# Three edge sweeps of a graph network: all rows gathered by GpSimd, and one multiplication for sixteen scaled copies

## The reference

```python
# layer 0 (1 head) and layer 1 (4 heads, with edge terms): attention
h = x @ W
alpha = leaky_relu(a_src[src] + a_dst[dst] (+ a_edge))
alpha = exp(alpha - segment_max(alpha, dst)[dst])
out   = segment_sum(alpha[:, None] * h[src], dst) / segment_sum(alpha, dst)
# layer 2: sums of edge attributes, then three dense layers
agg   = segment_sum(edge_attr_128, dst)
# layer 3: messages by relation
h     = einsum('nd,rdo->rno', x, W_rel)
agg   = segment_sum(h[edge_type, src], dst) / deg
```

## Time and profile before

| | us |
|---|---|
| median of 3 runs | 9807.24 (9797.97 to 9817.08) |
| span of the profiled execution | 9691.9 |
| first stage | 324.2 |
| sweep A, first gather to last join | 2242.5 |
| node stage after it | 384.0 |
| sweep B | 3141.5 |
| node stage after it | 434.2 |
| sweep R | 3012.6 |
| the rest | 152.9 |

### The profile page before, as it was taken

One profiled execution on the slowest core, in us unless ns is written; L12 is line 12 of the kernel. 1 busy time (PEld: TensorE's weight loads), 2 busy tenths in 40 slices (PEclk: granted clock), 3 DMA queues, 4 the chain that ended last, 5 costly groups with the idle time before them and its releaser, 6 DMA issues.

```text
span 9691.9 us, 57509 instructions
## 1 busy us (share of the span) xinstructions
PE 645.5 (7%) x2460; PEld 429.5 (4%) x2460; DVE 3381.8 (35%) x6204; ACT 1028.8 (11%) x3093; POOL 4970.1 (51%) x5237
## 2 busy tenths in 40 slices
PE   1100000000140000000000000580000000000000
PEld 1000000000140000000000000240000000000000
DVE  6555555555563222222222222761111111111113
ACT  1222222222120000000000000460000000000000
POOL 5766666666457444444444444216444444444445
PEclk7555555555565555555555555795555555555555
DMA  4456666666433222222222222452222222222222
GB/s 158 145 178 199 194 186 196 192 193 202 155 108 94 67 72 70 69 73 69 73 70 72 70 71 69 164 200 71 64 67 66 68 68 68 65 70 68 68 68 97
DMA packets 344911, 1045.34 MB, mean 108 GB/s; under 512 B 111529, under 2 KB 139564, under 8 KB 306594
## 3 DMA queue, kind: packets, MB, share of 16 engines
q1 hardware_dynamic: 157746, 670.54, 19.3%
q0 software_dynamic: 172192, 365.19, 14.8%
q10 hardware_dynamic: 14544, 5.93, 0.3%
HBM read 527.27 MB, written 513.96 MB: 107 GB/s over the span
## 4 chain that ended last, share of the span: by engine, by line
SPq 36%; issue 31%; DVE 14%; another core or an unknown queue 8%; PE 3%; POOL 3%; ACT 3%; ACTq 1%; DMA 1%; DVEq 0%; POOLq 0%
SPq L250 21%; SPq L249 7%; SPq L247 7%; DVE ps L1256 2%; DVE ps L1281 2%; POOL node_sums L1387 1%; DVE edge_rows L1286 1%; ACT edge_rows L1220 1%; DVE edge_rows L1264 1%; PE ps L2028 1%; ACTq L250 1%; DVE edge_logit L1356 1%; DVE feat_prod L1343 1%; DVE fine L592 1%
## 5 line engine op out<-in xcount | busy, mean ns | idle before, releaser
L1158 POOL DMA_INDIRECT edge_rows<-table_b,src_i x1523 | 1440.8, 946 | 1642.7 <-DMA sums_b<-edge_rows 1161.0
L2113 POOL DMA_INDIRECT edge_rows<-table_rel,rel_row x1523 | 1440.7, 946 | 1641.1 <-DMA sums_rel<-edge_rows 1096.3
L1158 POOL DMA_INDIRECT edge_rows<-table_a,src_i x1568 | 1485.0, 947 | 702.8 <-issue 487.3
L2197 DVE TENSOR_TENSOR edge_rows<-edge_rows,ps 128x1024 f32<-128x1024 f32 x195 | 237.9, 1220 | 2301.3 <-DMA edge_rows<-table_rel 2220.7
L1286 DVE TENSOR_TENSOR edge_rows<-edge_rows,ps 128x1032 f32<-128x1032 f32 (+1 forms) x390 | 484.2, 1241 | 962.5 <-remote 726.8
L1350 DVE TENSOR_TENSOR edge_rows<-edge_rows,ps 128x2112 f32<-128x2112 f32 (+1 forms) x99 | 230.9, 2332 | 1010.1 <-ACT ps L1223 961.8
L1220 ACT ACTIVATE edge_rows<-edge_rows,weight_decay 128x129 f32<-128x129 f32 x1560 | 493.6, 392 | 211.5 <-issue 211.3
L1281 DVE TENSOR_TENSOR ps<-edge_rows,ps 128x1032 f32<-128x1032 f32 (+1 forms) x390 | 485.6, 1245 | 8.6 <-issue 1.9
L1316 DVE TENSOR_TENSOR z<-edge_rows,dst_logit 128x16 f32<-128x16 f32 (+2 forms) x198 | 40.1, 203 | 1194.2 <-DMA edge_rows<-table_b 1171.4
L1223 ACT ACTIVATE ps<-weight_decay 128x128 f32<-128x128 f32 (+1 forms) x99 | 27.7, 280 | 3036.5 <-DVE weight_decay L1337 1562.8
L2144 ACT ACTIVATE ps<-keep 128x16 f32<-128x16 f32 x98 | 19.6, 201 | 2985.8 <-issue 1534.7
(11 more groups left out here) (296 smaller groups left out, 3207.3 us busy)
## 6 DMA issues: line engine op xcount, KB each, us to landing
sums_a<-edge_rows SPq DMA_DIRECT2D x98, 2064.0 KB
sums_b<-edge_rows SPq DMA_DIRECT2D x98, 1120.0 KB, 4.2
edge_rows<-in_ea SPq DMA_DIRECT2D x98, 1024.0 KB
sums_rel<-edge_rows SPq DMA_DIRECT2D x98, 1024.0 KB, 3.9
table_rel<-rel SPq DMA_DIRECT2D x98, 512.0 KB
edge_rows<-table_b SPq DMA_DIRECT2D x2880, 0.5 KB
edge_rows<-table_b ACTq DMA_DIRECT2D x2880, 0.5 KB
edge_rows<-table_rel ACTq DMA_DIRECT2D x2880, 0.5 KB
```

The source lines that it names most:

```text
L1158: e.indirect_dma_start(out=rows[:, s, i, 0:L.W], out_offset=None, in_=L.table, in_offset=bass.IndirectOffsetOnAxis(ap=src[:, at:at + 1], a ...
L2113: e.indirect_dma_start(out=rows[:, s, i, :], out_offset=None, in_=table_rel, in_offset=bass.IndirectOffsetOnAxis(ap=rel_row[:, at:at + 1], ...
```

## The change

`Helped` is gone with its tables, registers, transposes and semaphores; `Gathers`, in its place, only counts what POOL's gathers add to a buffer's semaphore. POOL gathers all 16 columns of every group in all three sweeps. In sweep A ScalarE now does as in sweep B: one exponential for weights and decays into PSUM, and VectorE multiplies all of a group's rows in one instruction. What orders the rest stays as it is.

```diff
-    def fetch(self, e, regs, g, p0, n):
-        ...
-            for p in range(p0, p0 + n, len(regs)):
-                m = min(len(regs), p0 + n - p)
-                e.load(regs[0:m], self.index[h:h + 1, p:p + m])
-                for i in range(m):
-                    row = e.snap(regs[i])
-                    e.dma_start(self.rows[p + i:p + i + 1, s, LAST, 0:self.W], self.table[bass.ds(row, 1), :]
-                                ).then_inc(self.fetched[h % 3].sem, 16)
...
# gpsimd, all sweeps
-                for i in range(GC - (g in helped.place)):
+                for i in range(GC):
...
# sync, sweep B (and the like in sweep R, and on scalar in both)
-                if L.AE:
-                    helped.fetch(e, regs_sync, g + 4, 0, P // 4)
-                    helped.fetch(e, regs_sync, g + 3, P // 4, P // 4)
...
# scalar, attention sweeps
-                    if H == 1:
-                        e.activation(at[:, 0, cols, :], at[:, 0, cols, :], ACT.Exp).then_inc(weight_exped.sem, 1)
-                        e.activation(factors[:, 1, cols, :], at[:, 1, cols, :], ACT.Exp).then_inc(exped.sem, 1)
-                        if part == 0:
-                            e.wait_ge(*weight_exped.at(g + 1))
-                            for i in range(first * GK, end * GK):
-                                done = e.activation(R[:, i, 0:NW], R[:, i, 0:NW], ACT.Copy, scale=wd[:, g % 2, 0, i, :])
-                            done.then_inc(weighted.sem, 1)
-                    else:
-                        e.activation(factors[:, :, cols, :], at[:, :, cols, :], ACT.Exp).then_inc(exped.sem, 1)
+                    e.activation(factors[:, :, cols, :], at[:, :, cols, :], ACT.Exp).then_inc(exped.sem, 1)
...
# vector, join
-                if H == 1:
-                    e.wait_ge(*weighted.at(g + 1))
...
# vector, attention sweeps
-                    if H > 1 or part == 1:
-                        weights = wd[:, b, 0, cols, :] if H == 1 else factors[:, 0, cols, :]
-                        ...
+                    weights = factors[:, 0, cols, :]
+                    now = heads(R)[:, cols, :, :]
+                    t_weight = then(e.tensor_tensor(now, now, bc(weights.unsqueeze(3), [P, (end - first) * GK, H, C + 1]),
+                                                    ALU.mult))
```

More of the change, by code:

```diff
@@ new lines, in build, with __init__, total, landed @@
+    class Gathers:
+        def __init__(self, NS):
+            self.NS = NS
+            self.first_half = sem_of("edges_first_half", 16 * GK)
+            self.slot = [sem_of(f"edges_gathered{i}", self.total(max(g for g in range(NG) if g % NS == i)))
+                         for i in range(NS)]
+        def total(self, g):
+            return 16 * GC * (g // self.NS + 1) - (16 * GK if g == NG - 1 else 0)
+        def landed(self, g, i):
+            return self.first_half if g == NG - 1 and i < GK else self.slot[g % self.NS]
+        def wait_half(self, e):
+            e.wait_ge(*self.first_half.at(16 * GK))
@@ L640, in edge_places @@
                 t = then(e.tensor_copy(tmp_e[:, :], src[:, :]))
-                then(e.memset(helped_f[:, :, :], 0.0))
-                e.wait_ge(*step.at(step.n))
-                e.tensor_copy(helped_f[:, 0, 0:len(helped_b)], helped_columns(tmp_e, helped_b)).then_inc(helped_floated.sem, 1)
                 e.wait_ge(*zero_stored.at(N_ZERO))
@@ L1107, in attention_edges @@
         summed = sem_of("edges_summed", NG)
-        helped = Helped(L.name, helped_b if L.AE else {}, helped_src, L.table, L.W, rows, NS, stored, summed)
-        gathered = [sem_of(f"edges_gathered{i}", helped.all_by_pool(i)) for i in range(NS)]
+        gathers = Gathers(NS)
         def parts(g):
@@ L1154, in gpsimd @@
                     e.wait_ge(*summed.at(g - NS + 2))
-                for i in range(GC - (g in helped.place)):
+                for i in range(GC):
                     at = natural(g, i)
-                    landed = helped.first_half if g == NG - 1 and i < GK else gathered[s]
                     e.indirect_dma_start(
@@ L1311, in vector @@
                     if g == NG - 1 and part == 0:
-                        e.wait_ge(*helped.first_half.at(16 * GK))
+                        gathers.wait_half(e)
                     else:
-                        e.wait_ge(*gathered[g % NS].at(helped.by_pool[g]))
-                        helped.wait(e, g)
+                        gathers.wait(e, g)
                     t_logit = then(e.tensor_tensor(z[:, b, ts, :, :], maxima[:, ts, :, :], logit[:, ts, :, :], ALU.add))
@@ L2093, in edges_rel_stage @@
         summed = sem_of("edges_summed", NG)
-        helped = Helped("rel", helped_b, helped_rel, table_rel, D, rows, NS, stored, summed)
-        gathered = [sem_of(f"edges_gathered{i}", helped.all_by_pool(i)) for i in range(NS)]
+        gathers = Gathers(NS)
         crossing = Crossing("cross", rows[:, (NG - 1) % NS, GC - GK:GC, :], sb("border_state", [P, NV + 1])[:, :],
@@ L2115, in gpsimd @@
                         in_offset=bass.IndirectOffsetOnAxis(ap=rel_row[:, at:at + 1], axis=0)
-                    ).then_inc(landed.sem, 16)
+                    ).then_inc(gathers.landed(g, i).sem, 16)
             for g in range(NG - NS, NG):
@@ L2179, in vector @@
                         e.wait_ge(*keep_copied.at(1))
-                        e.wait_ge(*gathered[0].at(helped.by_pool[0]))
+                        gathers.wait(e, 0)
                     keep_now = bc(ps[:, 4 + g % 2, t * GK:(t + 1) * GK].unsqueeze(2), [P, GK, D])
@@ L2191, in vector @@
                     if t == 0 and g == NG - 1:
-                        e.wait_ge(*helped.first_half.at(16 * GK))
+                        gathers.wait_half(e)
                     elif t == 0 or g == NG - 1:
-                        e.wait_ge(*gathered[s].at(helped.by_pool[g]))
-                        helped.wait(e, g)
+                        gathers.wait(e, g)
                     e.wait_ge(*step.at(done))
@@ L2283, in _ @@
         def _(e):
-            regs_sync.extend(e.alloc_register(f"row_sync{i}") for i in range(32))
             graph.sync(e)
@@ L2302, in _ @@
         def _(e):
-            regs_scalar.extend(e.alloc_register(f"row_scalar{i}") for i in range(32))
             graph.scalar(e)
```

56 lines of the change are left out of this document (3 added, 53 removed).

## The result

On the chip of this comparison the changed kernel takes 7935.3 us (median of 4 runs, 7927.7 to 7939.8), where the kernel before takes 9811.3 (4 runs, 9798.0 to 9817.1). The ratio is 0.809, with a 95% interval of 0.8075 to 0.8097. That is clearly faster, yet 295 us above the forecast of 7640 and 105 us above the end of its range, 7830.

What follows compares the result with a forecast made beforehand. SyncE's and ScalarE's issue of single-row fetches was taken to bound sweeps B and R, GpSimd's gathers coming next. 9807.2 - 2218.2 (B and R) + 48 (sweep A) = 7637, called 7640 us; range 7305 to 7830.

Steps and rivals of the forecast that it cites:

- B, first gather to last join: Sweep B without fetches: 1568 gathers at 1.251 us plus small extras and tail, 1970.6 us, a gain of 1170.9.
- R (7753.6 - 5581.2): Sweep R without fetches: GpSimd's gathers plus 4 us for landing and a short join, 1965.3 us, a gain of 1047.3.
- A (2549.9 - 339.6): Sweep A: its 2242.5 us grow by 48 as VectorE takes over the row weighing from ScalarE.
- the rest of the span: Profiled time outside the sweeps: no change; first-stage instructions removed there gain zero, at best 3 us.
- between span and median: Runs' median 115 us above the profiled span of 9691.9: kept, as if it all lay around the program.
- GpSimd's own step is next: Sweeps B and R: with fetches gone, GpSimd's gathers at 1.251 us each set the time; both gain 2218.2 us.
- Sweep A, +48 us: Sweep A: VectorE's twentieth instruction, at one in 1.40 us while GpSimd gathers, costs 0.5 us in each of 98 groups.
- R1: Sweep A: the 1.40 us bind ScalarE alone, so the sweep falls to 1970.6 us; 7317 in all, chance 0.22.
- R4: Sweeps B and R: stores' landing is the true limit, groups stay at 31 us, total within 20 of 9807; chance 0.01.
- R3: Sweeps B and R: scattered rows slow DMAs, gather step grows; slower than before once over 1.96 us; chance 0.02.
- R2: The 1.40 us and slow first fetches belong to the profiled execution alone, so 190 us less gain; 7779, chance 0.20.
- The rule against the change: Spreading DMAs over engines helps, so giving GpSimd back 90 gathers costs 113 us; 9920 us in all, chance 0.01.

Runs made afterwards that it cites:

- second kernel of the first batch: Kernel before without helped groups, its fetches gone, ScalarE's sixteen copies in sweep A kept; 7909.4 us, ratio 0.8171.
- first batch: Four edited kernels beside the kernel before (9687.6 us), on a held chip, one where gathers settle at one in 1.40 us.
- third batch: Changed kernel beside the kernel before on a free chip, where gathers keep 1.25 us: 7099.1 against 6984.7 us, ratio 1.0161.
- first batch's first kernel: Kernel before with sweep A's edit alone, VectorE weighing rows in one multiplication, row fetches kept; 9683.2 us, ratio 0.9998.

## Why the prediction was wrong, point by point

By its own sum, against the profile of the changed kernel on the chip of the result:

| term | forecast | measured | off by |
|---|---|---|---|
| B, first gather to last join (5128.6 - 2952.4) | 1970.6 | 2176.2 | +205.6 |
| R (7753.6 - 5581.2) | 1965.3 | 2172.4 | +207.1 |
| A (2549.9 - 339.6), 2242.5 before | 2290.5 | 2210.3 | -80.2 |
| the rest of the span, 1295.3 before | 1295.3 | 1356.0 | +60.7 |
| between span and median | 115.3 | 20.4 | -94.9 |

- **The bound was read rightly.** SyncE's and ScalarE's fetches set B and R on a held chip, and without them GpSimd does. The second kernel of the first batch has the whole gain from that edit alone. It was forecast as 2218.2 us and measured as 965.3 + 840.2 = 1805.5.
- **The step that failed is "GpSimd's own step is next", with 1.251 us.** Over B and R the gathers took a mean of 1.384 us, 1.400 after the first 180, which is the +412.7 us of the first two rows; the last three rows hide 114 of them and leave the total 298 us off. The 1.251 was read from the earlier trace rows, where GpSimd had just been idle 13.84 us, and from the earlier trace rows, at the start of a sweep. In both a held chip still has room for gathers, by the reservoir's description. The forecast knew the 1.40 us, saw it on ScalarE and VectorE and even wrote "while GpSimd gathers" beside it, but applied it to these two engines and not to GpSimd. Yet a row gave it away: 22.3 us a group in sweep A, close to 16 x 1.40 = 22.4. I split this mean into 20.0 of gathers and 2.3 of pauses for VectorE, and took the pauses for a cause. In four kernels, with nineteen or twenty instructions a group, the pauses changed in length and number and the mean stayed within 1%, so it is the rate that was fixed and not the pauses. Had I taken 22.3 us a group for B and R too, the sum would have been 9807 - 2218 + 2 x 98 x 2.3 = 8040 without sweep A's +48, 105 us above the result.
- **Sweep A, +48 us.** That VectorE takes ScalarE's place and that its twentieth instruction makes a long group 1.40 us longer came out as written, 28.03 us for 26.60. What failed is the way from the group to the sweep: the forecast let the other groups stay as they were, and fewer groups were long instead. The edit is worth nothing within 12 us on a held chip (ratio 0.9988 to 1.0008), and from first to last gather the sweep took 2188.6 us, 2187.8 before. What the table shows as -80 is a shorter tail after the last gather (21.7 us, 54.8 before) beside that wrong +48.
- **R1 (7317)** fell with the same measurement; with its copies gone the sweep kept its length. **R4** fell as well. **R3** was right that the step grows without pauses, and its sign, a step over 1.3 us, showed; the step is 1.40 and not over 1.96, and its reason is wrong, since neither half the rows nor half the bytes changed it.
- **R2, that the slowness belongs to the profiled execution alone,** fell: the other executions of the changed kernel took 4 to 12 us more than the profiled one, and in each batch the executions agree to 0.3%. What it suspected did turn out to be no property of the kernel. On a free chip neither the 1.40 us nor the long first fetches of the earlier trace rows exist, and even the steady 0.82 us for a fetch, on which both R2 and my sum rested, is 0.41. I named only the first two as suspect.
- **The rest of the span, +60.7 us,** is spread over the first stage (15.4), the two node stages (18.5 and 18.4) and the end (8.4). The forecast let it stay as it was. No run tells why it grew; the two traces need not be of one chip.
- **The rule against the change** had 0.01. The Trainium skill (Perfetto Trace Analysis, section DMA Optimizations) says that where generating descriptors is the bottleneck, spreading DMAs over the engines that can issue them may help. I worked out 90 gathers, 113 us. On the free chip of the third batch the rule holds, and 114 us was measured; on the held ones the trace disagrees with it, for the helpers were then slower than the helped engine. "Slower" had 0.03 in all; on the third batch's chip the time did get longer, by 1.6%.
- **The 115 us outside the span** were no such thing. The changed kernel's spans are 11 to 13 us below their times on this chip, and those of the kernel before about 5 us below in the first batch. The profile of before, 9691.9 us beside runs of 9798 us and more, must come from an execution quicker than those; it lies among the spans of the first batch's runs (9666.5 to 9693.3), so it need not come from the chip of the runs beside it.

**What remains open** is what the 1.40 us is. That the cause lies outside the kernel follows from one kernel's times of 9688 and 6981 with nothing changed. Whether it is the chip, what the chip is attached to, or a state that passes with time does not: the two held sets are the two earliest, and no chip was seen to be both. The chip of the result is not on record; the first batch's is another than the three free ones. The behaviour, a reservoir that fills and then empties at a fixed rate while GpSimd shows "issue" and no wait, is like what the Trainium skill (NOTIFIC — the notification-queue block, section 7.1) says of the path for trace records, that full inner buffers can stall an engine. No run here shows that it is this path; every execution has a recorded span, and it would take a held chip without records, which wasn't tried.

No version beats both kernels on both kinds. On the held chip of the first batch the kernel without helped groups and with ScalarE's copies (7909 us) is the best measured of what computes everything, and nothing shows it to differ from the changed one (its versions with half gathers took 7917 and 7918); on a free chip it is the kernel before.

## What to carry to other kernels

Take an engine's rate from a long stretch in which it never pauses, and compare mean distances from start to start over a whole sweep: a group of 22.3 us against 16 instructions of 1.25 us is a rate not yet explained, not a pause to be hidden. When equal instructions of several engines come at one odd distance with "issue" ahead of them, ask whether the machine or the kernel sets it, and measure the kernel before on a second chip ahead of removing work-sharing that the first one shows as too slow. A balance between queues (here 128 small DMAs against one gather) has a break-even price. Without help GpSimd needs 16 x 1.25 = 20.0 us a group. The helper needs some 5.0 for the store and the wait for a buffer, and 32 fetches: 18.3 us where a fetch takes it 0.41 and 31.4 where it takes 0.82. By this estimate help pays below (20.0 - 5.0) / 32 = 0.47 us a fetch, or 0.54 where the gathers take 22.4 us a group, and the sign of the change turns there.

## What the runs showed of the hardware

- The same kernel takes 9811 and 9688 us in the two earliest sets of runs and 6981 to 6996 in four later ones on three other chips, at nearly equal granted clock (0.53 to 0.54). Within a batch the runs agree to 0.3%. Of the first kind's extra 2682 us (spans 9679.3 of the first batch's first kernel, 6997.3 of the third batch's kernel before) 2460 lie in the three sweeps.
- GpSimd's gather of 128 rows has a step of 1.248 to 1.252 us on free chips for whole sweeps, 1.208 with 64 rows, 1.251 with rows half as wide (both from the held chip's first 174 to 225 us of sweep R). It is nearly all paid for the instruction.
- On held chips the gathers of B and R go on at 1.400 us each once some 19 of them are ahead of that rate. In sweep A, where VectorE or ScalarE has nineteen or twenty instructions a group, groups of 20.0 us alternate with groups of 19 or 20 times 1.40, at a mean of 1.405 to 1.414 us a gather in four kernels.
- A fetch of one row costs SyncE 0.41 us on a free chip. On a held one it costs 3.5 to 4.0 at a sweep's start, beside gathers without a pause, and 0.82 later.
